# Softmax attention of 16 heads in a decoder kernel: how two heads share the PSUM banks of the scores

## The reference

```python
scores = jnp.einsum('bhsk,bhtk->bhst', Q[..., :KPH], K) / math.sqrt(KPH)
attn = jax.nn.softmax(scores, axis=-1)
ao = jnp.einsum('bhst,bhtv->bhsv', attn, V)
ao = ao.transpose(0, 2, 1, 3).reshape(B, S, H * KPH)
ao = jnp.concatenate([ao, jnp.zeros((B, S, D - LAT), ao.dtype)], axis=-1)
mla_out = ao @ o_w + o_b
```

## Time and profile before

| | us |
|---|---|
| median of 3 runs | 1302.38 |
| lowest, highest | 1298.53, 1306.37 |
| the profiled execution | 1303.17 |
| its span | 1301.3 |

### The profile page before, as it was taken

The page is one execution under the profiler, slowest core; times in us unless marked ns, Lnnn a source line. Parts: engine busy times, 40 slices in busy tenths (PEclk is TensorE's granted clock), DMA queues, the critical chain, the costliest instruction groups (busy, mean ns, idle before and its releaser), DMA issues.

```text
span 1301.3 us, 17124 instructions
## 1 busy us (share of the span) xinstructions
PE 1161.3 (89%) x6126; PEld 614.8 (47%) x6126; DVE 914.4 (70%) x1753; ACT 876.4 (67%) x1130; POOL 618.7 (48%) x455
## 2 busy tenths in 40 slices
PE   5899999999999999987888888999989999976865
PEld 2444444444444444422222222677766777733444
DVE  5666667766776677568989896255547777678885
ACT  2799999999989998963777777445545665633411
POOL 3577777777767776884555551033320000044232
PEclk8999999999999999986999999899999999978778
DMA  7100000000000000100000000000010000000000
GB/s 188 50 1 1 1 1 1 1 1 1 1 0 1 1 1 1 65 1 17 2 1 1 2 1 2 1 1 1 1 61 1 1 1 1 1 1 1 0 9 25
DMA packets 25631, 14.48 MB, mean 11 GB/s; under 512 B 14558, under 2 KB 24396, under 8 KB 25420
## 3 DMA queue, kind: packets, MB, share of 16 engines
q1 hardware_dynamic: 25548, 13.39, 3.7%
HBM read 12.34 MB, written 1.05 MB: 10 GB/s over the span
## 4 chain that ended last, share of the span: by engine, by line
PE 36%; POOL 30%; issue 19%; DVE 13%; ACT 1%; POOLq 0%; DMA 0%; SPq 0%; ACTq 0%; DVEq 0%
DVE ARENA L1048 6%; POOL ARENA L2466 6%; POOL ARENA L2464 6%; POOL ARENA L2460 6%; PE PS L914 4%; PE PS L889 4%; POOL WQ L2477 3%; POOL ARENA L2490 3%; PE PS L803 3%; PE PS L1269 3%; PE PS L1258 2%; PE PS L1253 2%; PE PS L1245 2%; PE PS L770 2%; PE PS L754 2%
## 5 line engine op out<-in xcount | busy, mean ns | idle before, releaser
L2320 DVE TENSOR_SCALAR ARENA<-PS,ARENA 128x512 f32<-128x512 f32 x256 | 174.6, 744 | 67.8 <-PE PS L1954 67.3
L1048 DVE TENSOR_REDUCE ARENA<-PS 128x1 f32<-128x512 f32 x256 | 161.1, 683 | 27.2 <-PE PS L770 26.6
L959 ACT ACTIVATE ARENA<-PS 128x1024 f32<-128x1024 f32 x128 | 128.8, 1026 | 58.3 <-PE PS L789 58.0
L2133 ACT ACTIVATE ARENA<-ARENA 128x2048 f32<-128x2048 f32 x64 | 122.2, 1911 | 62.3 <-DVE ARENA L2320 61.8
L1954 PE MATMUL PS<-ARENA 64*128 64x512 f32 x512 | 130.9, 631 | 0.0
L2140 ACT ACTIVATE ARENA<-ARENA,consts_sb 128x2048 f32<-128x2048 f32 x64 | 124.6, 1994 | 0.4
L1964 PE MATMUL PS<-ARENA 128*64 128x512 f32 x512 | 118.7, 606 | 1.3 <-issue 1.3
L2146 ACT ACTIVATE ARENA<-ARENA 128x2048 f32<-128x2048 f32 x64 | 118.3, 1897 | 0.0
L1204 POOL TENSOR_TENSOR ARENA<-ARENA 128x512 f32<-128x512 f32 x32 | 40.6, 1270 | 142.0 <-DVE ARENA L1162 141.9
L2473 POOL TENSOR_SCALAR WQ<-ARENA,consts_sb 128x512 bf16<-128x512 f32 x32 | 22.3, 695 | 159.8 <-DVE ARENA L2296 159.8
L770 PE MATMUL PS<-ARENA 32*128 32x512 bf16 x256 | 74.3, 405 | 25.7 <-DVE ARENA L1048 21.4
(11 more groups left out here) (279 smaller groups left out, 2693.6 us busy)
## 6 DMA issues: line engine op xcount, KB each, us to landing
ARENA<-in_window_bias_dram SPq DMA_DIRECT2D x1, 1536.0 KB, 6.8
WKVG<-in_L_attn_W_in_dram SPq DMA_DIRECT2D x3, 448.0 KB, 5.5
X<-in_x_dram SPq DMA_DIRECT2D x4, 256.0 KB, 4.4
W<-in_L_ffn_w_dram SPq DMA_DIRECT2D x1, 1024.0 KB
out_dram<-X SPq DMA_DIRECT2D x4, 256.0 KB, 2.3
BV<-in_L_attn_b_in_dram SPq DMA_DIRECT2D x1, 512.0 KB, 6.1
Wout<-in_L_attn_W_out_dram SPq DMA_DIRECT2D x1, 512.0 KB, 4.8
WQ<-in_L_attn_wq_dram SPq DMA_DIRECT2D x1, 512.0 KB, 3.3
```

The lines of the kernel that those rows point to most:

```text
L959: act.activation(PT[m % PT_SLOTS], bank(("cP", m)), ACT.Exp, scale=0.5).then_inc(sem("c_exp"), 1)
L1048: dve.tensor_reduce(NMX[:, w % 2, t, h:h + 1], bank(("cS", n, j)), AX.X, ALU.max, negate=True).then_inc(sem("c_max"), 1)
L2133: act.activation(chunk(u, half), chunk(u, half), ACT.Sqrt).then_inc(sem("rooted"), 1)
L2320: dve.tensor_scalar(D[:, u % 2, kt, hd, :], bank(("S", u, c)), K2[:, u % 2, kt, hd:hd + 1], 1e-30, ALU.add, ALU.max).then_inc(sem("guarded ...
```

## The change

The first pass now takes both heads of a step in one job of two banks: both matmuls, then one reduce over 2 x 512 columns that writes two maxima. The pool cS becomes banks 0 to 3, cV4 bank 4, and cP banks 5 to 7. In cP, the shifted scores of each head are a job of one bank, with an exponential of 512 columns each. The projections cQK become two jobs of one bank each, with a wait of its own ahead of each evacuation. On PE both score matmuls of a step come ahead of the shifted ones. Counts on semaphores follow (c_max once a step, c_exp twice).

```diff
+def heads_job(w, pool):
+    return [(("cQK", w, side), 1, [("c_v32", 2 * w + side + 1)], pool) for side in range(2)]
...
-            jobs += [(("cQK", u - 29), 2, [("c_v32", 2 * (u - 29) + 2)], "A")]
+            jobs += heads_job(u - 29, "A")
...
         if n < CSTEPS:
-            jobs += maxima(n, 0)
+            jobs += [(("cS", n), 2, [("c_max", n + 1)], "cS")]
         if 0 <= n - CLAG < CSTEPS:
-            jobs += [(("cP", n - CLAG), 2, [("c_exp", n - CLAG + 1)], "cP")]
-        if n < CSTEPS:
-            jobs += maxima(n, 1)
+            jobs += [(("cP", n - CLAG, j), 1, [("c_exp", 2 * (n - CLAG) + j + 1)], "cP") for j in range(2)]
...
-"cS": range(0, 3), "cV4": range(3, 4), "cP": range(4, 8)}
+"cS": range(0, 4), "cV4": range(4, 5), "cP": range(5, 8)}
...
-                r = slice(32 * (2 * pair + j), 32 * (2 * pair + j) + 32)
-                done(pe.matmul(begin(("cS", n, j)), STK[r, w % 4, 0, t * P:(t + 1) * P], STK[r, w % 4, 1, :],
-                               start=True, stop=True), ("cS", n, j))
+                o = begin(("cS", n))
+                for j in range(2):
+                    r = slice(32 * (2 * pair + j), 32 * (2 * pair + j) + 32)
+                    mm = pe.matmul(o[:, j, :], STK[r, w % 4, 0, t * P:(t + 1) * P], STK[r, w % 4, 1, :],
+                                   start=True, stop=True)
+                done(mm, ("cS", n))
...
-                o = begin(("cP", n))
                 for j in range(2):
                     r = slice(32 * (2 * pair + j), 32 * (2 * pair + j) + 32)
-                    mm = pe.matmul(o[:, j, :], STK[r, w % 4, 1, kt * P:(kt + 1) * P], STK[r, w % 4, 0, :],
-                                   start=True, stop=True)
-                done(mm, ("cP", n))
+                    o = begin(("cP", n, j))
+                    done(pe.matmul(o, STK[r, w % 4, 1, kt * P:(kt + 1) * P], STK[r, w % 4, 0, :],
+                                   start=True, stop=True), ("cP", n, j))
...
                 if n < CSTEPS:
-                    maxima(n, 0)
+                    maxima(n)
                 if 0 <= n - CLAG < CSTEPS:
                     shifted(n - CLAG)
-                if n < CSTEPS:
-                    maxima(n, 1)
...
             for side in range(2):
                 c = side * GROUPS + g
-                act.activation(V32[:, side], bank(("cQK", w))[:, side, :], ACT.Identity,
+                full(act, ("cQK", w, side))
+                act.activation(V32[:, side], bank(("cQK", w, side)), ACT.Identity,
                                bias=BQK[:, c:c + 1]).then_inc(sem("c_v32"), 1)
...
-                    act.activation(PT[m % PT_SLOTS], bank(("cP", m)), ACT.Exp, scale=0.5).then_inc(sem("c_exp"), 1)
+                    for j in range(2):
+                        full(act, ("cP", m, j))
+                        act.activation(PT[m % PT_SLOTS][:, j, :], bank(("cP", m, j)), ACT.Exp, scale=0.5
+                                       ).then_inc(sem("c_exp"), 1)
...
-                dve.tensor_reduce(NMX[:, w % 2, t, h:h + 1], bank(("cS", n, j)), AX.X, ALU.max,
+                dve.tensor_reduce(NMX[:, w % 2, t, 2 * pair:2 * pair + 2], bank(("cS", n)), AX.X, ALU.max,
                                   negate=True).then_inc(sem("c_max"), 1)
```

More of the change, by code:

```diff
@@ L270, in prepare @@
     def prepare(w):
-        return (values_of(w // GROUPS) if w % GROUPS == 0 else []) + [(("cQK", w), 2, [("c_v32", 2 * w + 2)], "cP")]
-    def maxima(n, j):
-        return [(("cS", n, j), 1, [("c_max", 2 * n + j + 1)], "cS")]
+        return (values_of(w // GROUPS) if w % GROUPS == 0 else []) + heads_job(w, "cP")
     for n in range(CSTEPS + 20):
         if n < CSTEPS:
-            jobs += maxima(n, 0)
+            jobs += [(("cS", n), 2, [("c_max", n + 1)], "cS")]
         if 0 <= n - CLAG < CSTEPS:
-            jobs += [(("cP", n - CLAG), 2, [("c_exp", n - CLAG + 1)], "cP")]
-        if n < CSTEPS:
-            jobs += maxima(n, 1)
+            jobs += [(("cP", n - CLAG, j), 1, [("c_exp", 2 * (n - CLAG) + j + 1)], "cP") for j in range(2)]
         if prepared(n) is not None:
@@ L439, in stage_f_jobs @@
     return jobs + [(("fD", steps - 1), 1, [("x_final", steps)])]
-POOLS = {"all": range(BANKS), "D": range(0, 6), "DO": range(6, 8), "A": range(0, 6), "PV": range(6, 7), "out0": range(7, 8), "cS": range(0, 3), "cV4": range(3, 4), "cP": range(4, 8)}
+POOLS = {"all": range(BANKS), "D": range(0, 6), "DO": range(6, 8), "A": range(0, 6), "PV": range(6, 7), "out0": range(7, 8), "cS": range(0, 4), "cV4": range(4, 5), "cP": range(5, 8)}
 def place_jobs(jobs):
@@ L751, in prepare_heads @@
             pe.wait_ge(sem("xt_ready"), norm_no(2, b))
-            o = begin(("cQK", w))
             for side in range(2):
-                mm = pe.matmul(o[:, side, :], WX[:, side, g, :], XT[:, b], start=True, stop=True)
-            done(mm, ("cQK", w))
+                o = begin(("cQK", w, side))
+                done(pe.matmul(o, WX[:, side, g, :], XT[:, b], start=True, stop=True), ("cQK", w, side))
         def tensor_c(pe, begin, done, ln_turn, tail):
@@ L761, in prepare, with maxima @@
                 prepare_heads(pe, begin, done, w)
-            def maxima(n, j):
+            def maxima(n):
                 w, i = divmod(n, 8)
@@ L799, in values @@
                 o = bank(("cV4", w))
-                pe.wait_ge(sem("c_exp"), 8 * w + 2 * kt + 2)
+                pe.wait_ge(sem("c_exp"), 2 * (8 * w + 2 * kt + 2))
                 for h in range(4):
@@ L935, in heads_out @@
             act.wait_ge(sem("expand_cols"), 1)
-            full(act, ("cQK", w))
             if w:
@@ L1041, in take_values, with maxima @@
                 ins.then_inc(sem("c_v"), 1)
-            def maxima(n, j):
+            def maxima(n):
                 w, i = divmod(n, 8)
                 t, pair = divmod(i, 2)
-                h = 2 * pair + j
-                full(dve, ("cS", n, j))
-                dve.tensor_reduce(NMX[:, w % 2, t, h:h + 1], bank(("cS", n, j)), AX.X, ALU.max,
+                full(dve, ("cS", n))
+                dve.tensor_reduce(NMX[:, w % 2, t, 2 * pair:2 * pair + 2], bank(("cS", n)), AX.X, ALU.max,
                                   negate=True).then_inc(sem("c_max"), 1)
             def split_maxima(w):
-                dve.wait_ge(sem("c_max"), 16 * w + 16)
+                dve.wait_ge(sem("c_max"), 8 * w + 8)
                 part = [TMX[:, w % 2].rearrange("p t (j r) -> p t j r", r=32)[:, :, :, 24 + k] for k in range(3)]
@@ L1185, in stack @@
             if w >= 4:
-                full(pool, ("cP", 8 * (w - 4) + 7))
+                for j in range(2):
+                    full(pool, ("cP", 8 * (w - 4) + 7, j))
             pool.tensor_tensor(STK[:, w % 4], R1, MID, ALU.subtract).then_inc(sem("c_stack"), 1)
```

1 line of the change is left out of this document (removed).

## The result

| | before | changed |
|---|---|---|
| median of 7 runs each, us | 1302.94 | 1315.13 |
| lowest, highest | 1298.53, 1306.37 | 1306.25, 1317.10 |
| the profiled execution, its span | 1303.17, 1301.3 | 1317.1, 1315.1 |
| granted clock of PE, mean over that span | 0.949 | 0.938 |

The changed kernel is slower by 0.8%: the ratio is 1.0081, with an interval of 1.006 to 1.0101. The forecast was 1303.0, and 1315.13 lies above the range of 1292 to 1310. The seven runs of the changed kernel differ among themselves by the clock: 1306.25 at a mean of 0.947, 1309.4 and 1309.5 at 0.943, the others 1315 to 1317 at 0.938 or 0.939.

The account below looks back on a forecast made before the run. An ordinary window was taken as bound by a loop through PE, DVE and ACT, not by DVE alone. Terms -0.7 +1.2 -1.4 +1.5 summed to +0.6 us, giving a median of 1303.0; 80% range 1292 to 1310.

Parts of the forecast that it names:

- One exponential 0.60, one reduce 1.22: Estimated prices in us of a 512-column exponential on ACT and of a 1024-column reduce for two heads on DVE.
- the rival by which ACT costs more: Second rival: a half-wide exponential costs 0.685 us and the three banks hold PE longer; 1309 us, chance 0.12.
- (4,1) is held by the exponential of (3,0): Shifted scores, step 4's second head, wait for the exponential of step 3's first: 715.59 against 715.63, ACT wait replacing DVE's.
- -0.11 of the first four reduces: Steps 0 and 1 of an ordinary window: two merged reduces take 2.36 us instead of 2.47.
- the -0.04 at (4,1): Step 4's second head: value products behind it, and step 5 behind them, gain 0.04 us and no more.
- the stretch of step 5's exponentials and the copy: On ACT in an ordinary window: two half-wide exponentials ahead of the value-bank copy add 0.07 us to the loop.
- Ordinary window 12.6 to 12.8: Length in us of a window without a batch's end; -0.08 each, -0.7 for the nine in the middle.
- The first rival: DVE is the bound after all: windows of about 11.9 to 12.0 us, 1292 us in all; chance 0.17.
- the third: Third rival: score and shifted matmuls no longer run side by side, 12 windows 12 us slower, 1315; chance 0.03.
- Batch windows 0.3 to 0.5 longer, +1.2 for three: Windows with a batch's end: step 2's shifted pair goes out later, +0.32, and +0.07 for step 5, three times.
- The beginning -1.4: Stretch from 566 to 645 us: 13 pairs of reduces in the chain of waits gain 0.11 us each.
- The tail +1.5 (0.5 to 3): Stretch from 802 to 822 us, no scores left: three banks delay value products and half-wide exponentials show, +1.5 us.

Follow-up runs that it names:

- e1: Changed kernel with score matmuls of the batch windows and of two steps near 643 us issued again; median 1308.2 us, ratio 1.004.
- e6: Kernel before, with ACT's copy of the turned outputs and evacuation of the output projection ahead of their step's exponential; 1294.79 us, ratio 0.9955.
- e2: Changed kernel, with ACT's copy of the turned outputs and evacuation of the output projection ahead of their step's exponentials; 1299.4 us, ratio 0.9973.
- e11: e2 with six banks instead of three for the shifted scores once no scores are left; 1299.29 us, ratio 0.9976.
- e12: Kernel before with only PE's order changed, both score matmuls of a step ahead of the shifted ones; 1306.96 us, ratio 1.0037.
- e3: Kernel before with only the shifted scores in single banks (four of them) and one exponential a head; 1306.74 us, ratio 1.0027.
- e7: Kernel before with both ACT reorderings, batch-end instructions and value-bank copy ahead of the exponentials; 1288.6 us, ratio 0.9912.
- e9: e8 with the value products of steps 4 and 6 put between the two shifted heads of their step on PE; 1288.68 us, ratio 0.99.
- e4: Changed kernel with the copy of the value bank ahead of step 5's exponentials on ACT; 1300.07 us, ratio 0.9975.
- e5: Kernel before with the copy of the value bank ahead of step 5's exponential on ACT; 1294.0 us, ratio 0.9939.
- e8: Changed kernel with both ACT reorderings, batch-end instructions and value-bank copy ahead of the exponentials; 1300.02 us, ratio 0.9991.
- e10: e7 with the value products of steps 4 and 6 ahead of the second score matmul on PE; 1296.01 us, ratio 0.9962.

## Why the prediction was wrong

Point by point:

- *One exponential 0.60, one reduce 1.22.* Right (0.600 and 1.220). That rules out the rival by which ACT costs more: it decides from 0.68. The 1309 that it gave is nearer to the result than the forecast, but its mechanism is not there. ACT's busy time in a window was to be about 10.1 and is 10.30. (0.60 and 0.50 against 1.02 make 0.08 and not 0.07, a slip that changes nothing.)
- *(4,1) is held by the exponential of (3,0).* Right, the step on which the forecast rested. After, the time line of PE has

```profile
719.90 0.38 PE L790 MATMUL PS<-ARENA 32*128 32x512 bf16 x1 [0.39 <-ACT ARENA L958]
...
721.21 0.39 PE L770 MATMUL PS<-ARENA 32*128 32x512 bf16 x2
722.39 0.39 PE L790 MATMUL PS<-ARENA 32*128 32x512 bf16 x1 [0.43 <-ACT ARENA L958]
723.40 1.07 PE L803 MATMUL PS<-ARENA 128*32 128x512 f32 x8 [0.62 <-issue]
```

  The wait for DVE of the earlier trace rows at 715.63 has become one for ACT, 8.32 after step 7 (711.58 to 719.90) against 8.42 (707.21 to 715.63). Step 5 is still 0.10 earlier (9.63 against 9.73, from 716.94 of the earlier trace rows), and the value products behind the copy are 0.02 later (11.82 against 11.80, from 719.01). So the -0.11 of the first four reduces is there (step 3 comes 7.14 after step 7 instead of 7.25), the -0.04 at (4,1) is +0.01, and the stretch of step 5's exponentials and the copy costs 0.12 where +0.07 stood. The wait at (6,1) is in no step of the forecast.
- *Ordinary window 12.6 to 12.8.* 12.81 measured, so -0.08 was +0.02: the nine windows give nothing where -0.7 stood. DVE's busy time was to fall to 10.9 and is 11.25; its idle time rose to 1.56, not 1.8: a merged reduce saves 0.05 in a window's busy time (0.42 by eight), about half of what was put there. The first rival, DVE as the bound, is refuted by that idle time, and so is the third: score and shifted matmuls still start within 0.01 us (724.39 and 724.40, 739.20 and 739.20). That the third gave 1315, the time measured, is chance.
- *Batch windows 0.3 to 0.5 longer, +1.2 for three.* Right in kind, and a little over the range: +0.55 in the window shown, by the copy L963 ahead of step 3 (0.50) and, not foreseen, by the evacuation L972 ahead of step 5 (0.31).
- *The beginning -1.4.* The projections at 637 are 0.8 earlier; the clock's first fall, at 647, costs 1.4 and turns that into +0.6. In e1's profile, without that fall, the next projections (652.89) are 1.1 earlier than before's, so the term was nearly right and the fall costs 1.7.
- *The tail +1.5 (0.5 to 3).* 41.36 us from the output projection of the third batch to the router before, 43.32 after, +2.0, inside the bounds. But the clock is at half for 10.2 us of it before and 8.9 after, and e1, which has the changed kernel's tail with the fall only at 821.1, needs 40.8; so the agreement may be luck. With both orders alike on ACT e6 needs 37.5 and e2 40.5, with half clock for none of it and for 3.4 us. The waits for banks are there (e11), but what they cost isn't separated from the clock.

The step that failed is the sum of +0.6. It priced each stretch by its waits alone and took PE's rate as given. The earlier trace rows has a granted clock of 1.00 in both windows and 0.81 in the beginning, so the clock was in view as something that moves, and no term and no rival asked what 0.4 us of new waits at the end of a batch do to it. That missing term is the largest of all: twice 3.2 us behind batch windows and 1.4 at 647, together 7.8 of 13.8 us of the profiled execution, with 1.3 more in the router at a lower clock. e1's profile shows it as the cause, and not only as a companion, of the losses behind the batch windows: with the added waits left in the windows and PE kept at work, the clock stays and the loss goes. Its median, 6.9 us below the changed kernel's although PE does more, says the same more weakly, since half of its executions keep a lower mean clock. e2 shows the other way to the same end. The router's 1.3 is not of that kind: e1 has it too. Nor is it shown that the 1.9 behind the gate belong to the change: no run touches the code there, and it takes from 470.4 (e12) to 475.1 us (e3) in the profiles, 473.1 before and 475.0 after.

What stays open: why the clock falls behind one batch window and not behind another of the same code (e12), whether a mere shift in time of the same waits would move a fall (no run tests that, and the changed kernel's own executions range from 0.938 to 0.947), the 2 us of the tail, and the 1.9 behind the gate. A version with the single reduce alone was not tried, since two pairs of banks for the scores and two for the shifted ones do not fit in eight banks with cV4; the reduce's own worth is known only from the ordinary window, where it brings step 3 forward by 0.11 and the window's end by nothing. Both the best kernels here, e7 without the change (1288.6) and e9 with it (1288.7), beat the kernel before by 1%, by orders on ACT and PE. They differ in PE's order too. Like with like, by medians beside which the kernel before has 1302.0 to 1303.0, the change costs 4.6 us with the batch's instructions first on ACT (e2 against e6), 6.1 with the copy first (e4 against e5) and 11.4 with both (e8 against e7), and gains 7.3 with the value products ahead as well (e9 against e10). So its sign depends on the orders around it.

## What to carry to other kernels

Where a period is a loop through several engines, making the busiest cheaper buys idle time; look first at what stands in front of a short instruction that frees a bank, as a copy behind two exponentials did here (0.6 us of every ordinary window, for one moved line). And when a change adds waits of some tenths to TensorE ahead of its densest work, read the granted clock of the stretch behind and price a fall as well as the wait: here 3.2 us against 0.55. Compare two orders by several executions and their clocks, since one kernel's runs differed by 11 us with the clock.

## What the runs showed of the hardware

The clock fell without any long pause of PE. In the batch window before the fall at 739 the waits on PE's time line are 0.22 to 0.63 us each (the longest at 738.18), and PE is busy 12.24 of 14.81 us. The kernel before, with 12.33 of 14.26 in its own, kept the clock, although one of its waits, at 733.27, is 1.24 us long. So the longest single wait did not decide it. The Trainium skill ("TensorE: Matmul & The Clock Gate", section A second HAM failure mode: psum-queue depth-cycling) describes a kernel with PSUM banks used in turns, in which short idle times of PE between groups of matmuls make the clock go back and forth; the trace agrees in kind, with three falls of 6.8 us each in the middle of the stage.

Matmuls that add nothing to the result can shorten a kernel: e1's profiled execution is 13.6 us shorter than that of the same kernel without them, its median 6.9. A half-wide exponential costs 0.600 against 1.02, and two in a row 1.08 to 1.09 from start to end, so the second costs 0.49: splitting costs ACT 0.07 a pair, as estimated.
